# A graph and attention network on one core: node features fetched after counting has begun, one block turned in the next stage, the last score tile and the output products reordered

## What is computed

```python
edge_index = jnp.stack([src, dst])                                # 41250 edges, sorted by dst
x = x + gnn0(layernorm(x))    # x @ wc + mean over edges of (x @ wn)[dst] + bias
x = x + ffn0(layernorm(x))    # causal attention, 8 heads of 64, then 8 experts mixed by a gate
x = x + gnn1(layernorm(x))    # self and neighbour products, layer norm, affine
x = x + ffn1(layernorm(x))    # 3-tap convolution, qkv, softmax over the top 16 scores of each row, wo
```

## Time and profile before

| | us |
|---|---|
| runs shown | 1590.02, 1593.36, 1597.71 |
| median | 1593.36 |
| the profiled execution, its own time | 1593.47 |
| its span in the profile | 1591.7 |
| busy: PE, DVE, ACT, POOL | 1450.2, 1004.5, 722.5, 646.1 |

### The profile page before, as it was taken

One profiled execution on the slowest core, in us unless ns is written; L12 is line 12 of the kernel. 1 busy time (PEld: TensorE's weight loads), 2 busy tenths in 40 slices (PEclk: granted clock), 3 DMA queues, 4 the chain that ended last, 5 costly groups with the idle time before them and its releaser, 6 DMA issues. The chain is left out here.

```text
span 1591.7 us, 22280 instructions
## 1 busy us (share of the span) xinstructions
PE 1450.2 (91%) x8144; PEld 898.6 (56%) x8144; DVE 1004.5 (63%) x1879; ACT 722.5 (45%) x1406; POOL 646.1 (41%) x533
## 2 busy tenths in 40 slices
PE   4888999988888899999999899979999988998998
PEld 2554545446666654454545554546686776776664
DVE  7997254347777702123213321768999999999994
ACT  4442114335656511111111230155788787788783
POOL 4787100045656300000000043016876775776763
PEclk9999999999999999989999999989999999999999
DMA  7001000073122060000000110003011101101001
GB/s 246 2 1 83 0 1 1 0 197 69 35 57 45 1 241 0 0 0 1 0 0 0 42 38 0 1 11 83 1 36 33 34 9 27 33 2 34 1 1 65
DMA packets 28604, 57.03 MB, mean 36 GB/s; under 512 B 7936, under 2 KB 12676, under 8 KB 28240
## 3 DMA queue, kind: packets, MB, share of 16 engines
q1 hardware_dynamic: 27184, 53.03, 12.1%
q10 hardware_dynamic: 1312, 2.56, 0.4%
HBM read 28.77 MB, written 5.84 MB: 22 GB/s over the span
## 5 line engine op out<-in xcount | busy, mean ns | idle before, releaser
L1479 POOL TENSOR_TENSOR tl_ex<-tl_ex,tl_left 128x1250 f32<-128x1250 f32 x80 | 209.8, 2623 | 30.4 <-ACT tl_left L1814 25.7
L1298 DVE SCALAR_TENSOR_TENSOR X<-ex_ps_x,g,X 128x512 f32<-128x512 f32 x80 | 59.9, 750 | 194.3 <-PE ex_ps_x L1191 194.3
L1983 POOL TENSOR_TENSOR lo<-xn,hi 128x512 f16<-128x512 f32 x5 | 5.9, 1188 | 377.3 <-ACT hi L2087 377.3
L1619 PE MATMUL tl_banks<-identf,tl_ex 128*128 128x128 f32 x800 | 134.2, 282 | 24.1 <-ACT tl_pt L1835 14.3
L1835 ACT COPY tl_pt<-tl_banks 128x512 f32<-128x512 f32 (+1 forms) x200 | 108.3, 541 | 91.7 <-PE tl_banks L1619 91.1
L1191 PE MATMUL ex_ps_x<-w,hid 128*128 128x512 f32 (+1 forms) x320 | 144.8, 605 | 0.0
L1164 PE MATMUL ex_ps_h<-yt,w 128*128 128x512 f32 (+1 forms) x384 | 143.3, 527 | 0.0
L1244 ACT ACTIVATE hid<-ex_ps_h,b 128x512 f32<-128x512 f32 (+1 forms) x48 | 29.1, 608 | 245.0 <-PE ex_ps_h L1164 245.0
L1619 PEld LDWEIGHTS tl_banks<-identf,tl_ex 128*128 128x128 f32 x800 | 88.9, 141 | 86.2 <-issue 45.0
L1905 DVE MAX8 tl_m<-tl_banks 128x8 f32<-128x1250 f32 x80 | 116.3, 1454 | 10.0 <-PE tl_banks L1589 9.9
L1911 DVE MAX8 tl_m<-tl_left 128x8 f32<-128x1250 f32 x80 | 117.1, 1464 | 2.8
(11 more groups left out here) (281 smaller groups left out, 2996.8 us busy)
## 6 DMA issues: line engine op xcount, KB each, us to landing
kl<-KT SPq DMA_DIRECT2D x16, 320.0 KB, 4.4
qs<-QO SPq DMA_DIRECT2D x16, 320.0 KB, 6.1
tl_kl<-tl_KT SPq DMA_DIRECT2D x16, 320.0 KB, 4.4
tl_qs<-tl_QO SPq DMA_DIRECT2D x16, 320.0 KB, 6.0
w<-in_L_ffn_W SPq DMA_DIRECT2D x8, 512.0 KB
w<-in_L_ffn_W SPq DMA_DIRECT2D x4, 1024.0 KB, 8.6
at_kept<-AT SPq DMA_DIRECT2D x1, 3200.0 KB, 9.0
AT<-at_kept SPq DMA_DIRECT2D x1, 3200.0 KB, 18.3
```

What stands on the lines that cost most here:

```text
L1479: pool.tensor_tensor(ex[:, n % EXS, 0:N], ex[:, n % EXS, 0:N], left[:, n % LEFT, :], ALU.subtract).then_inc(s_probs, 1)
L1619: mm = pe.transpose(ps_t[:, b * P:(b + 1) * P], ex[:, n % EXS, a + b * P:a + (b + 1) * P], m.identf[:, :])
```

## The change

1. **Nodes.** ScalarE issues the transfers of `x` when `s_used` is 2, behind tile 0 of the count, instead of when the edges are in. `INVERT_AT` goes from 60 to 66, and the three tables of the node work move five tiles later.
2. **Last block.** `graph_in` no longer turns block 9. `graph_causal` turns it ahead of `gather(0)` into banks 5 to 7, ScalarE keeps it there, and the gather waits for it only at its tenth node tile.
3. **Last score tile.** Its leftover exponentials are taken in two halves, and VectorE subtracts both halves, not GpSimd.
4. **Output products.** `begin(8)` and `begin(9)` do three of the four products of row tiles 8 and 9 inside the loop, in banks 4 and 5 (the other tiles share banks 0 to 3), and the fourth products of tiles 3 to 7 stand elsewhere.

```diff
-INVERT_AT = 60
+INVERT_AT = 66
-        return [j for j in range(NT) if c == min((min((j + 1) * P, N) - 1) // CD, NC - 1)]
+        return [j for j in range(NT - 1) if c == min((min((j + 1) * P, N) - 1) // CD, NC - 1)]
-    rows_at = {66 + 24 * t: t for t in range(NT)}
-    cols_at = {70 + 24 * t: t for t in range(NT)}
-    own_at = {75 + 24 * t + 5 * k: (t, k) for t in range(NT) for k in range(KD)}
+    rows_at = {71 + 24 * t: t for t in range(NT)}
+    cols_at = {75 + 24 * t: t for t in range(NT)}
+    own_at = {80 + 24 * t + 5 * k: (t, k) for t in range(NT) for k in range(KD)}
...
             act.wait_ge(s_zeroed, 1)
-            act.wait_ge(s_edges, 16 * 2 * (EG + 1))
+            act.wait_ge(s_used, 2)
             for a in (0, 3, 6):
...
+        ps_f = banks[:, 5:8, :].rearrange("p b c -> p (b c)")
...
                     for t in range(NT):
+                        if t == NT - 1:
+                            pe.wait_ge(s_flip_kept, 1)
                         for part in (hi, lo):
...
+            for a in range(NT):
+                mm = pe.matmul(ps_f[:, a * P:(a + 1) * P], m.AT[:, a, (NT - 1) * P:NP], m.ident16[:, :],
+                               start=True, stop=True)
+            mm.then_inc(s_flipped, 1)
             gather(0)
...
+            act.wait_ge(s_flipped, 1)
+            act.activation(m.A[:, NT - 1, :], ps_f[:, 0:NP], ACT.Copy, accum_out=m.deg_d[:, NT - 1:NT]
+                           ).then_inc(s_flip_kept, 1)
             keep_sum(0)
...
-                if 0 <= n - 1 < TN:
+                if 0 <= n - 1 < TN - 1:
                     subtract(n - 1)
...
+            def free_bank(t):
+                b = 1 if t >= EARLY or t % 4 == 3 else 0
+                pe.wait_ge(s_exp, TN - 1 + b)
+                pe.wait_ge(s_read, TN - 1 + b)
+
+            def begin(t):
+                pe.wait_ge(s_normed, (TN - 2 * NT) // 2)
+                free_bank(t)
+                for k in range(HP - 1):
+                    pe.matmul(proj_bank(t), QO[:, k, t * P:(t + 1) * P], wo[:, k, :], start=(k == 0), stop=False)
...
+                if n == TN:
+                    begin(EARLY)
+                elif n == TN + 1:
+                    project(3)
+                    project(4)
+                elif n == TN + 2:
+                    project(6)
+                    project(7)
                 if 0 <= back < TN:
                     turn(back, 1)
...
                 elif n == TN:
+                    begin(EARLY + 1)
                     project(2)
-                    project(3)
                 elif n == TN + 1:
-                    project(4)
                     project(5)
-            for t in range(6, NT):
+            for t in range(EARLY, NT):
                 project(t)
...
-                act.activation(lf, lf, ACT.Exp, bias=negm[:, n:n + 1]).then_inc(s_rest, 1)
+                for a, b in ([(0, N)] if n < TN - 1 else HALVES):
+                    act.activation(lf[:, a:b], lf[:, a:b], ACT.Exp, bias=negm[:, n:n + 1]).then_inc(s_rest, 1)
...
+            last = TN - 1
+            dve.wait_ge(s_exp, TN)
+            for v, (a, b) in enumerate(HALVES):
+                dve.wait_ge(s_rest, TN + v)
+                dve.tensor_tensor(ex[:, last % EXS, a:b], ex[:, last % EXS, a:b], left[:, last % LEFT, a:b], ALU.subtract
+                                  ).then_inc(s_last, 1)
```

More of the change, by code:

```diff
@@ L399, in _ @@
                                 flip(j)
-                for c0, j in flips_at[ET - 1]:
+                for c0, j in flips_at.get(ET - 1, ()):
                     pe.wait_ge(s_drained, c0 + 1)
@@ L543, in graph_causal @@
          s_o_d, s_spilled, s_gathered, s_sum_v, s_sum_a, s_near, s_biased, s_owned, s_sums, s_deg, s_added, s_seen,
-         s_aggr, s_dev, s_step) = s.signals(
+         s_aggr, s_dev, s_step, s_flipped, s_flip_kept) = s.signals(
             "rows turned_x cols gained q_ps k_ps v_ps sq summed root inv qn qk_turned qk_kept v_kept fetched_0 "
             "fetched_1 staged staged_k scored masked maxed exp inverse probs_d probs_p turned kept_a kept_d weighed o_a o_d "
-            "spilled gathered sum_v sum_a near biased owned sums deg added seen aggr dev step")
+            "spilled gathered sum_v sum_a near biased owned sums deg added seen aggr dev step flipped flip_kept")
         s_fetched = (s_fetched_0, s_fetched_1)
@@ L1341, in top_layer @@
     EARLY = 8
+    HALVES = [(0, BANK), (BANK, N)]
     for b in range(KD):
@@ L1359, in top_layer @@
          s_fetched_0, s_fetched_1, s_staged, s_scored, s_max, s_negm, s_read, s_max2, s_topped, s_exp, s_rest,
-         s_sum, s_inv, s_blank, s_probs, s_turned, s_kept, s_weighed, s_drained, s_normed, s_biased,
+         s_sum, s_inv, s_blank, s_probs, s_last, s_turned, s_kept, s_weighed, s_drained, s_normed, s_biased,
          s_projected, s_final, s_stored) = s.signals(
             "zn_a zn_p x_turned x_kept_a x_kept_v edge tapped mid conv first first_kept job job_kept shifted wo_in added "
-            "fetched_0 fetched_1 staged scored max negm read max2 topped exp rest sum inv blank probs turned kept "
+            "fetched_0 fetched_1 staged scored max negm read max2 topped exp rest sum inv blank probs last turned kept "
             "weighed drained normed biased projected final stored")
@@ L1403, in proj_bank @@
         def proj_bank(t):
-            return banks[:, t % 6, :]
+            return banks[:, t % 4 if t < EARLY else t - EARLY + 4, :]
         def chunk_tiles(c):
@@ L1610, in turn @@
             def turn(n, g):
-                if g == 0:
+                if n == TN - 1:
+                    pe.wait_ge(s_last, min(g, 1) + 1)
+                elif g == 0:
                     pe.wait_ge(s_probs, n + 1)
@@ L1676, in job @@
                     mm.then_inc(s_job, 1)
+            def free_bank(t):
[7 more added lines that the diff above has]
+                    pe.matmul(proj_bank(t), QO[:, k, t * P:(t + 1) * P], wo[:, k, :], start=(k == 0), stop=False)
             def project(t):
                 pe.wait_ge(s_normed, (TN - NT + t) // 2 + 1)
[L1680 to L1689, removed]
+                if t < EARLY:
+                    free_bank(t)
+                    if t >= 4:
+                        pe.wait_ge(s_final, t - 3)
+                pe.matmul(proj_bank(t), QO[:, HP - 1, t * P:(t + 1) * P], wo[:, HP - 1, :], start=(t < EARLY), stop=True
+                          ).then_inc(s_projected, 1)
             pe.wait_ge(s_blank, 1)
```

## The result

| | before | after |
|---|---|---|
| median (runs) | 1593.65 (10) | 1601.14 (10) |
| lowest, highest | 1590.02, 1597.71 | 1597.70, 1605.38 |
| profiled execution, its own time | 1593.47 | 1603.89 |
| its mean granted clock | 0.979 | 0.972 |

The ratio is 1.0048, with a 95% interval from 1.0037 to 1.0059: the change makes the kernel 7.6 us slower, between 5.9 and 9.4. The forecast was 1602.0, with a range from 1596 to 1606.

What follows compares the result with a forecast made beforehand. The node chain through ScalarE was taken to bound the first flip, by 0.46 us over the count, and TensorE the end. Terms 11.3 - 1.5 - 1.4 + 0.1 + 0.1 = +8.6 us on 1593.47 gave 1602.0, range 1596 to 1606.

Steps and rivals of the forecast that it cites:

- S: When TensorE starts to count behind its branch: taken as 16.5 us, between 13.0 and 17.69.
- first mean: ScalarE's first mean of the late nodes, predicted at 27 us (S + 10.5), against 15.73 before.
- shift of the count: The count ends later by the node chain's whole delay: +11.3 us, between +7.8 and +12.5.
- slow clock at the start: TensorE resumes at 1.2 GHz after standing still before flip(0): +0.1 us, bounds 0 and +1.6.
- tables later: Node work five tiles later, inversion six: last product still ahead of the count's end, no instruction added, zero.
- block 9: At the seam, ten products and one copy leave the end of graph_in, so the gather starts sooner: -1.5 us.
- clock at the seam: A shorter pause before the gather regains half the slow-clock loss: -1.4 us, bounds 0 and -2.75.
- last tile and products: At the end, tile change zero; products fill two 0.68 us gaps but add 1.5 us idle: +0.1 (-1.4 to +1.5).
- Nodes later: At the start, late transfers delay ScalarE's means and the copies behind them, stopping TensorE at chunk 3 and flip(0): +11.3 us.
- the rival of a short branch: TensorE's branch becomes as short as VectorE's 1.53 us: S 13.0, total +5.1 us, 1598.6; chance 0.20.
- The count made up: Middle of the count runs faster with node work spread otherwise, some 5 us back: +3.6, 1597; chance 0.10.
- Faster: The node chain did not hold the first flip, only the count's start matters: about 1587; chance 0.07.

Runs made afterwards that it cites:

- a_edges: The changed kernel with the node transfers issued again when the edges are in, all else kept; median 1589.71, ratio 0.9972.
- b_nodes: The kernel before plus only the late node transfers and the tables five tiles later (INVERT_AT 66); median 1603.35, ratio 1.0062.
- a_used10: The changed kernel with the node transfers issued behind tile 8 of the count instead of tile 0; median 1603.28, ratio 1.0059.
- a_shortvar: The changed kernel with each of the first layer's variance passes reading 8 columns, not 512; median 1598.89, ratio 1.0035.
- b_seam: The kernel before plus only block 9 turned in graph_causal; median 1591.83, ratio 0.9981.
- a_edges_again: The same kernel as a_edges, run again on the chip of a_spread; median 1591.04, ratio 0.9975.
- a_late: The changed kernel with the mean at tile 46, variance at 58 and 70, inversion at 84, tables from 96; median 1592.00, ratio 0.9981.
- a_late_inverse: a_late with VectorE's inversion at tile 104 instead of 84 and the tables behind it from 114; median 1592.82, ratio 0.9979.
- a_late_inverse_edges: a_late_inverse with the node transfers issued early again, when the edges are in; median 1594.72, ratio 0.9997.
- a_spread: a_late_inverse with ScalarE's means and variances cut into single passes, every second tile from 46 to 84; median 1588.78, ratio 0.9961.
- b_tail: The kernel before plus only the last score tile on VectorE and the products ahead; median 1592.97, ratio 1.0005.
- b_shortvar: The kernel before with each of the first layer's variance passes reading 8 columns, not 512; median 1594.20, ratio 0.9998.

## Why the prediction was right

| step | predicted | measured |
|---|---|---|
| S, start of the count | 16.5 (13.0 to 17.69) | 16.25; 15.55 to 16.50 in the other late fetches |
| first mean | 27.0 | 27.08 |
| shift of the count | +11.3 | flip +11.34, last copy +10.94 |
| slow clock at the start | +0.1 (0 to +1.6) | -0.4, flip to last copy |
| tables later | 0 | within the same -0.4 |
| block 9 | -1.5 | -1.52 |
| clock at the seam | -1.4 (0 to -2.75) | -1.2, by luck |
| last tile and products | +0.1 (-1.4 to +1.5) | -0.16 |
| sum | +8.6 | +8.1 |

*Nodes later.* Right in mechanism and size. The chain through ScalarE's list ended last, by 0.46 us, so the whole delay went through. a_edges and b_nodes show that it is this part, a_used10 and a_shortvar that it is this chain. The ratios put the cost of the part at 0.0076 between a_edges and after, 12 us, and at 9.9 us in b_nodes.

*S.* The chosen value was a quarter of a microsecond too high, and half of one against the seven late fetches, which start at 16.04 on average. With the early transfers beside it TensorE's stall was 6.00 to 6.17 us in seven kernels; without them 4.62, 4.21, 4.08, 4.68, 4.36, 4.76 and 4.08. So the transfers add some 1.7 us, and 4.1 to 4.8 remain: the rival of a short branch, as short as VectorE's 1.53, is out. The Trainium skill (Runtime: NRT & Kernel Launch, "Instruction fetch mechanics") has a taken branch wait for a fetch when its target is not loaded; the packets of the instruction queues between 12 and 16 us agree with it:

```profile
q8 instruction: 1, 0.02, 2.3%
q14 instruction: 1, 0.01, 0.8%
```

In slices of 0.2 us the larger packet runs in 14.8 to 15.0 in the kernel before, where the packets of `x` are just running out, and in 13.2 to 13.4 in the changed one, with no packet of `x` beside it. TensorE starts some 3 us behind the start of that slice in both. So the whole gain lies ahead of the packet, where the prediction had looked for it. What fills the rest, behind the packet above all, no run here shows.

*Clock at the start.* TensorE stood longer than the prediction had it, 6.75 and 7.23 us and not most of 8. The changed kernel's clock is 0.50 from 30 to 40 and 0.55 from 40 to 50 us, far longer at the low level than before, and yet the stretch from the flip to the last copy is 0.4 us shorter; in a_edges, with the same tables and the early fetch, it is 103.00. b_nodes has the same two waits (6.45 and 7.23) and the same late tables, and there this stretch is 103.96 us, 0.8 longer than before. So what the term costs is between nothing and 0.8 us as far as these single executions tell; +0.1 fits, but wasn't measured to a tenth. That the full buffers make it cheap is argued, not shown.

*Block 9.* Right to 0.02 us in the changed kernel. In b_seam, a_edges and a_shortvar, where the ten products ran at the low clock, it was 1.13; in a_used10 and a_edges_again, where they didn't, 1.60.

*Clock at the seam.* The size was right (-1.2 for -1.4), the reason given isn't borne out: that a shorter pause brings the clock back sooner. With the short pause the low stretch lasted 3.4 us (after, a_edges, a_edges_again and a_shortvar) or 6.8 (b_seam), and there was none up to 160 us in a_used10, a_late, a_late_inverse, a_late_inverse_edges and a_spread. With the long pause it lasted 6.8 (before, b_tail) or 3.4 (b_shortvar and b_nodes, in the last from 150.8 on, 0.6 behind the gather's start). The two sets overlap, though none of the four with the long pause was without one. So -1.2 is what these two executions show, not a price of the change, and that it came near -1.4 is luck.

*The end.* Cost nothing, as said, but the parts differ. The prediction counted two idle gaps of 0.68 us and missed the third, at 1574.15, which the change keeps as one of 0.77. The 1.49 was foreseen. The gaps add up to 0.2 us more than before and the stretch is 0.16 shorter; the remaining 0.4 us weren't traced.

*The sum and the medians.* The terms make +8.1; the profiled executions differ by 10.4. The missing 2.3 us lie between gather and tail, where the same instructions run: 1420.39 us from 138.75 to 1559.14, and 1421.53 from 148.17 to 1569.70, though the second had 1.2 us less of slow clock in it. The ten executions of either kernel spread over 7.7 us. The ratio's +7.6 is the better figure and holds the sum well within its interval.

*The other rivals.* The count made up for nothing (a middle shorter by 0.4 us, not 5). "Faster" needed the node chain to have slack; it had none, and a_late shows the kernel in which that rival is true: the flip is at 30.18 once the nodes don't stand ahead of the copies. The prediction leaned a little to "slower" (0.50, with the line at 0.5%) over "the same" (0.42). The ratio is 0.48% and its interval runs from 0.37% to 0.59%: the kernel is slower than before, but on which side of that line isn't told.

## What to carry to other kernels

When a fetch is moved later, look in the list of the engine that uses it for what stands behind the use, and at who waits for that: here it wasn't the nodes that were missed but the bank copies queued behind them on ScalarE. An in-order engine turns late data of one chain into late work of another. The remedy is the same as the diagnosis: put the optional work behind the copies, and in pieces no longer than the slack of the engine that waits. And subtract two traces mark by mark (issue, first use, first flip, last copy, gather): what stays constant from which mark names the chain, with one execution of each.

## What had not been expected

TensorE's branch stall doesn't vanish: it is 4.08 to 4.76 us with the DMA engines idle but for the instruction packets, against 1.53 us on VectorE in the same place, and 6.00 to 6.17 us beside 2.5 MB of transfers. Removing one wait twice uncovered the next of the same kind: 7.23 us at the first flip, then 7.3 at VectorE's inversion with 5.33 at the second flip behind it, then 2.16. And the low clock at the seam comes and goes between kernels with the same instructions there, from none over 3.4 to 6.8 us.
